# The back of a unit in another order: both turned halves copied ahead of the Silu pair, the centred product in one stage, squares summed by ScalarE

## The reference

```python
x = x + conv_ref(_ln_c(x), ...)        # the mixer, a Mamba block
t = t + ffn_ref(_ln_t(t), ...)         # mixture of 8 experts, top 1, with capacity 640

# conv_ref
x_norm = layer_norm(x_flat, ln_g, ln_b)
y = mamba_block(x_norm, ...)           # in_proj, conv of 4 taps, silu, delta = softplus(...), selective scan
                                       # with 16 states for each of 128 channels, times silu(z), out_proj
y = layer_norm(y + skip_scale * x_norm, ln_g, ln_b)
y = y @ proj_w.T + proj_b

# ffn_ref
logits = x @ gate_w + gate_b
probs = softmax(logits); idx = argmax(probs)
pos = running count of tokens of the same expert - 1;  kept = pos < C
y = expert MLP of the kept tokens, times prb
```

## Time and profile before

| | |
|---|---|
| median of 3 runs | 411.19 us (409.86 to 411.86) |
| the profiled execution | 404.2 us, of which 402.4 us are its span |
| granted clock of PE, mean | 0.866 of full speed |
| pass 1 (scans from 95.54 us) | rests on 100 to 172 us |
| pass 2 | some 172 to 237 us |
| pass 3 | 237.25 to 288.42 us |
| the last unit's scans | 289.6 to 311.4 us |

### The profile page before, as it was taken

The page is one execution under the profiler, slowest core; times in us unless marked ns, Lnnn a source line. Parts: engine busy times, 40 slices in busy tenths (PEclk is TensorE's granted clock), DMA queues, the critical chain, the costliest instruction groups (busy, mean ns, idle before and its releaser), DMA issues. The chain is left out here.

```text
span 402.4 us, 4213 instructions
## 1 busy us (share of the span) xinstructions
PE 314.5 (78%) x1257; PEld 187.1 (47%) x1257; DVE 316.0 (79%) x355; ACT 225.2 (56%) x398; POOL 269.3 (67%) x196
## 2 busy tenths in 40 slices
PE   8832988647988799898888959877678759999930
PEld 3311433113634355473434426544366536989920
DVE  4799998999997968999797899999997223565650
ACT  4456688718676944857885846455533226464410
POOL 3436847988564797688659768966588500777771
PEclk9975799998899955969996896999999559999975
DMA  5186999989987866588975638999801063000000
GB/s 105 29 290 242 266 294 402 374 201 377 368 261 285 241 197 252 195 247 280 329 241 187 222 135 281 284 329 340 156 21 31 15 189 81 9 16 17 21 11 0
DMA packets 43985, 78.67 MB, mean 195 GB/s; under 512 B 16051, under 2 KB 26094, under 8 KB 43963
## 3 DMA queue, kind: packets, MB, share of 16 engines
q1 hardware_dynamic: 41066, 73.88, 57.4%
q0 software_dynamic: 2896, 4.53, 4.0%
HBM read 72.30 MB, written 7.54 MB: 198 GB/s over the span
## 5 line engine op out<-in xcount | busy, mean ns | idle before, releaser
L481 POOL TENSOR_TENSOR prod<-h,csb 128x1024 f32<-128x1024 f32 (+1 forms) x64 | 142.0, 2221 | 55.5 <-DVE h L1217 33.4
L1217 DVE TENSOR_TENSOR_SCAN h<-dA,Bp 128x1024 f32<-128x1024 f32 (+1 forms) x64 | 137.7, 2151 | 4.8 <-ACT hl L661 1.4
L910 PE MATMUL Yp<-prod,ident 128*128 128x512 f32 (+1 forms) x256 | 128.3, 633 | 16.1 <-POOL prod L481 16.0
L647 ACT ACTIVATE dA<-delta,aneg 128x1024 f32<-128x1024 f32 (+1 forms) x64 | 69.0, 1090 | 29.8 <-DVE h L1217 25.5
L910 PEld LDWEIGHTS Yp<-prod,ident 128*128 128x128 f32 x256 | 50.0, 209 | 73.9 <-issue 46.5
L1187 DVE TENSOR_TENSOR Bp<-Cp,bsb 128x1024 f32<-128x1024 f32 (+1 forms) x64 | 74.6, 1166 | 3.5 <-DMA bsb<-bc_rows 1.4
L562 POOL DMA_INDIRECT out_dram<-dA,csb x30 | 30.7, 1023 | 28.1 <-DVE dA L1404 20.8
L520 POOL DMA_INDIRECT slots<-rows_,slot x30 | 30.1, 1005 | 7.2 <-issue 4.5
L1390 DVE TENSOR_TENSOR dA<-Bp,b2s 128x320 f32<-128x320 f32 x8 | 3.9, 491 | 26.2 <-PE Bp L1081 26.2
L1071 PE MATMUL Cp<-prod,w1s 128*128 128x384 f32 (+1 forms) x64 | 21.5, 459 | 0.0
L1081 PEld LDWEIGHTS Bp<-w2s,prod 128*128 128x128 f32 x160 | 19.0, 192 | 1.4 <-ACT prod L814 1.0
(11 more groups left out here) (276 smaller groups left out, 552.1 us busy)
## 6 DMA issues: line engine op xcount, KB each, us to landing
bsb<-bc_rows SPq DMA_DIRECT2D x48, 512.0 KB, 5.6
csb<-bc_rows SPq DMA_DIRECT2D x48, 512.0 KB, 5.8
bsb<-bc_rows SPq DMA_DIRECT2D x16, 384.0 KB, 4.7
csb<-bc_rows SPq DMA_DIRECT2D x16, 384.0 KB, 5.7
slots<-fill POOLq DMA_DIRECT2D x1, 2600.0 KB, 21.8
csb<-slots SPq DMA_DIRECT2D x6, 325.0 KB, 5.4
bcs<-bc_rows SPq DMA_DIRECT2D x2, 512.0 KB, 12.3
xs_in<-in_x_dram SPq DMA_DIRECT2D x1, 768.0 KB, 5.5
```

The costliest lines, as they stand in the source:

```text
L481: po.tensor_tensor(prod[:, k % 4, c], h[:, k % 3, c], csb[:, k % CSLOTS, c], ALU.mult).then_inc(s_pP, 1)
L647: ac.activation(dA[:, k % 3, c], at(delta, UNITS[v][0])[:, c], ACT.Exp, scale=aneg[:, n:n + 1]).then_inc(s_dA, 1)
L910: ins = te_.matmul(Yp[:, c], idn, prod[:, k % 4, c], start=False, stop=(n == 15), skip_group_check=True)
L1217: ve.tensor_tensor_scan(h[:, k % 3, c], dA[:, k % 3, c], Bp[:, c], 0.0, ALU.mult, ALU.add).then_inc(s_scan, 1)
```

## The change

For the units 0, 1 and 2 (`v < CARRY`) the helper `parts` puts both halves into one stage. ACT copies both halves of the first transposes in stage 5, ahead of the Silu pair; on PE the transposes of the second half and `add_state(v, 4)` come ahead of the first matmul of B and C in stage 5. The second copy of the second transposes (L690) moves ahead of `front`'s work of stage 9 on ACT. The centred product of all 8 tiles is made in stage 10 in one bank (`products_bank`), and its squares and copies follow in ACT's stage 10. The logits of these units go to `M1` (`logits`), and the wait for the raw gate's second copy moves from PE to DVE (L1250). In every unit ACT sums the squares itself: one activation with an accumulator output for each tile of 64 channels, in the place of one activation for 8 or 4 tiles and a reduce on DVE (L1231, L1245, both gone). The second inverse root moves from stage 13 to stage 12.

```diff
+        def products_bank(v, q, m):
+            if v < CARRY:
+                return M1[:, 4 * q * C:(4 * q + m) * C]
+            return turn_bank(v, q)[:, 0:m * C]
+        def parts(v, n, first):
+            if v < CARRY:
+                return (0, 1) if n == first else ()
+            return (n - first,) if n in (first, first + 1) and quad(v, n - first) else ()
+        def logits(v, nt):
+            return (M1 if v < CARRY else M0)[:, 0:nt * E]
...
@@ ScalarE, back @@
                 if n == 2:
                     act.wait_ge(b_op, v + 1)
-                    ac.activation(sq[:, 0:nt, :], tiles(mixer_bank(v)[:, 0:nt * C], C, nt), ACT.Square).then_inc(b_sq, 1)
+                    for t in range(nt):
+                        ins = ac.activation(sq[:, t, :], mixer_bank(v)[:, t * C:(t + 1) * C], ACT.Square, accum_out=bs[:, 0, t:t + 1])
+                    ins.then_inc(b_sq, 1)
...
-                if n in (5, 6) and quad(v, n - 5):
-                    q, w = n - 5, quad(v, n - 5) * P
+                for q in parts(v, n, 5):
+                    w = quad(v, q) * P
                     act.wait_ge(b_tr, quads(v) + q + 1)
...
-                if n in (10, 11) and quad(v, n - 10):
-                    q, m = n - 10, quad(v, n - 10)
-                    act.wait_ge(b_lg, quads(v) + q + 1)
-                    src = tiles(turn_bank(v, q)[:, 0:m * C], C, m)
-                    ac.activation(sq[:, 4 * q:4 * q + m, :], src, ACT.Square)
+                for q in parts(v, n, 10):
+                    m = quad(v, q)
+                    act.wait_ge(b_lg, quads(v + 1) if v < CARRY else quads(v) + q + 1)
+                    src = tiles(products_bank(v, q, m), C, m)
+                    for t in range(m):
+                        ac.activation(sq[:, 4 * q + t, :], src[:, t, :], ACT.Square, accum_out=bs[:, 10, 4 * q + t:4 * q + t + 1])
                     ac.activation(cg[:, 4 * q:4 * q + m, :], src, ACT.Copy).then_inc(b_cg, 1)
-                if n == 13:
-                    act.wait_ge(b_var3, v + 1)
+                if n == 12:
+                    act.wait_ge(b_cg, quads(v + 1))
                     inverse_root(10, nt).then_inc(b_rs3, 1)
...
@@ ScalarE, the loop over the stages @@
-                    if v and n < 8:
+                    if v and n != 8 and n < 10:
                         back(v - 1, n)
                     if v + 1 < B:
                         front(v + 1, n)
-                    if v and n >= 8:
+                    if v and (n == 8 or n >= 10):
                         back(v - 1, n)
...
@@ TensorE, the loop over the stages @@
                 for n in range(16):
+                    if n == 5:
+                        if v:
+                            back(v - 1, n)
+                        add_state(v, n - 1)
                     if v + 1 < B:
                         front(v + 1, n)
...
+                    if n == 5:
+                        continue
...
@@ VectorE, back @@
-                if n == 2:
-                    dve.wait_ge(b_sq, v + 1)
-                    ve.reduce_sum(bs[:, 0, 0:nt], sq[:, 0:nt, :], X).then_inc(b_var, 1)
...
-                if n == 12:
-                    dve.wait_ge(b_cg, quads(v + 1))
-                    ve.reduce_sum(bs[:, 10, 0:nt], sq[:, 0:nt, :], X).then_inc(b_var3, 1)
                 if n == 13:
                     link = Chain(dve, b_dve, v, 3)
                     dve.wait_ge(b_lgt, v + 1)
                     dve.wait_ge(b_rs3, v + 1)
+                    if v + 2 < B:
+                        dve.wait_ge(f_zr, 2 * (v + 2))
```

More of the change, by code:

```diff
@@ L230, in metaformer_layer @@
         s_mul, s_dA, s_scan, s_pP, s_sum, s_hl = map(sem, "s_mul s_dA s_scan s_pP s_sum s_hl".split())
-        (b_yg, b_op, b_sq, b_y2, b_var, b_rs, b_n2, b_tr, b_n2T, b_pr, b_t1, b_tr3, b_h3T, b_lg, b_cg, b_var3, b_rs3,
+        (b_yg, b_op, b_sq, b_y2, b_rs, b_n2, b_tr, b_n2T, b_pr, b_t1, b_tr3, b_h3T, b_lg, b_cg, b_rs3,
          b_lgt, b_h3, b_ld, b_ex, b_oh, b_base, b_acc, b_pos, b_prb, b_ids, b_idx, b_dve, b_dve2, b_dve3, b_res,
          b_sent) = map(sem, (
-             "b_yg b_op b_sq b_y2 b_var b_rs b_n2 b_tr b_n2T b_pr b_t1 b_tr3 b_h3T b_lg b_cg b_var3 b_rs3 "
+             "b_yg b_op b_sq b_y2 b_rs b_n2 b_tr b_n2T b_pr b_t1 b_tr3 b_h3T b_lg b_cg b_rs3 "
              "b_lgt b_h3 b_ld b_ex b_oh b_base b_acc b_pos b_prb b_ids b_idx b_dve b_dve2 b_dve3 b_res b_sent").split())
@@ L675, in back @@
                 if n == 3:
-                    act.wait_ge(b_var, v + 1)
+                    act.wait_ge(b_sq, v + 1)
                     inverse_root(0, nt).then_inc(b_rs, 1)
@@ L797, in _ @@
                 decay_last(n)
-            for n in (5, 6, 8, 9, 10, 11, 13, 14, 15):
+            for n in (5, 6, 8, 9, 10, 11, 12, 14, 15):
                 back(CARRY, n)
@@ L824, in dense_hidden @@
                               bias=b1c[:, j:j + 1]).then_inc(d_hid, 1)
-            for n in (2, 3, 5, 8, 10, 13, 14):
+            for n in (2, 3, 5, 8, 10, 12, 14):
                 back(LAST, n)
@@ L956, in back @@
                     ins.then_inc(b_tr3, 1)
-                if n in (10, 11) and quad(v, n - 10):
-                    q = n - 10
+                for q in parts(v, n, 10):
                     pe.wait_ge(b_h3T, quads(v + 1) if v < CARRY else quads(v) + q + 1)
-                    if q == 1 and v < CARRY:
-                        pe.wait_ge(b_cg, quads(v) + 1)
                     for t in range(quad(v, q)):
-                        ins = te_.matmul(turn_bank(v, q)[:, t * C:(t + 1) * C], bT[0:C, (4 * q + t) * P:(4 * q + t + 1) * P],
+                        ins = te_.matmul(products_bank(v, q, quad(v, q))[:, t * C:(t + 1) * C],
+                                         bT[0:C, (4 * q + t) * P:(4 * q + t + 1) * P],
                                          cen[:, :], start=True, stop=True)
@@ L966, in back @@
                 if n == 12:
-                    if v + 2 < B:
-                        pe.wait_ge(f_zr, 2 * (v + 2))
-                    if v == CARRY:
+                    if v <= CARRY:
                         pe.wait_ge(b_cg, quads(v + 1))
@@ L973, in back @@
                     for t in range(nt):
-                        ins = te_.matmul(M0[:, t * E:(t + 1) * E], bT[0:C, t * P:(t + 1) * P], ggw[:, :], start=True,
+                        ins = te_.matmul(logits(v, nt)[:, t * E:(t + 1) * E], bT[0:C, t * P:(t + 1) * P], ggw[:, :], start=True,
                                          stop=True)
@@ L1249, in back @@
                     dve.wait_ge(b_rs3, v + 1)
-                    link(ve.tensor_tensor(work(1, nt), work(0, nt), over(bs[:, 12, 0:nt], E), ALU.mult))
+                    if v + 2 < B:
+                        dve.wait_ge(f_zr, 2 * (v + 2))
+                    link(ve.tensor_tensor(work(1, nt), logits(v, nt).rearrange("p (t e) -> p t e", e=E),
+                                          over(bs[:, 12, 0:nt], E), ALU.mult))
                     link(ve.tensor_tensor(work(2, nt), work(1, nt), gb[:, :].unsqueeze(1).broadcast_to([P, nt, E]), ALU.add))
```

## The result

| | before | changed |
|---|---|---|
| median | 407.54 us (405.61 to 411.86, 14 runs) | 415.35 us (411.84 to 417.52, 14 runs) |
| ratio | 1 | 1.0176 [1.014, 1.0213] |
| profiled execution, span | 402.4 us | 414.5 us |
| mean granted clock of PE | 0.866 | 0.841 |

The change makes the kernel slower by 7.8 us. The forecast was +5.0 us on a median of 411.19; the 14 runs of the kernel before, three of which were the ones shown, have a median of 407.54.

The account below looks back on a forecast made before the run. No engine is full, so the order of waits bounds it, with PE's clock. Terms: +6.2 us by pass 2 (pass 1's +2 included), -1.2 in pass 3, so +5.0 on the 411.19 median: 416 us, range 405.5 to 421.

Parts of the forecast that it names:

- A: Stages 5 and 6: PE starves and its clock falls there; 416 us, between 413.5 and 422; chance 0.48.
- Some 7: DVE's wait at the residual, in us, if PE's clock falls; 4.6 if the clock holds.
- the residual is late by 1.6 + 1.7 + 1.0 = 4.3: Stages 5 to 8, us: first B and C copy late 1.6, slower projection 1.7, slower step-size matmul 1.0.
- the 6 us: Lateness of the step size's second half; half caught up, leaving the expert choice 3.7 late, some 2 reaching the next pass.
- Rival C: Stages 10 to 14: 2.19 us gap gone, PE stays at full speed if later idle is below some 2; 406 us; chance 0.24.
- The stall ahead of the gate's second half: PE idle for 4.9 us, waiting for ACT's first raw gate copy behind the squares; the clock taken to fall.
- the chosen 0.4: Price in us of one ACT square with accumulator, chosen between 0.15 and 0.6; eight take 3.2 us.
- If the squares cost under 0.2 us: ACT's squares: a sign that the prediction would be wrong; 0.4 us apiece was assumed.
- The cover of stage 2: 2.6 us more on ACT for squares, hidden by its 1.71 us wait for PE; uncovered, up to 2 us a pass.
- 3.7 late: Choice of the expert after stages 9 to 12: 160.6 against 156.9 us.
- The reduces: DVE's two removed reduces per unit: gain 1.2 us in pass 3, nothing in passes 1 and 2 or the last unit.
- PE's list: Stage 5: adding ahead of B and C gains PE nothing, as it was waiting for Silu then anyway.

Follow-up runs that it names:

- e1: Changed kernel with stage 5 as before on both ACT (second half copied behind the Silu pair) and PE (old list): ratio to the kernel before 0.9825.
- e2: Kernel before with only the stage 5 edit (both halves copied early, PE's new order): ratio to the kernel before 1.0265.
- e3: Changed kernel plus three useless matmuls of 512 columns on PE between the two halves of B and C: ratio to the kernel before 0.988.
- a2: Changed kernel, unedited, measured again on another chip: ratio to the kernel before 1.0155.
- e10: Changed kernel with the whole of stage 5 as before, repeated on another chip: ratio to the kernel before 0.9899, 402.64 us.
- e5: Changed kernel with stage 5 as before, and ACT's first raw gate copy moved ahead of the squares: ratio to the kernel before 0.9847.
- e6: Kernel before with only ACT's second copy of the second transposes moved ahead of front's stage 9 work: ratio 0.9837, from two executions.
- e4: Changed kernel with one activation for all squares, DVE's reduces and the second root in stage 13 as before: ratio to the kernel before 1.0205.
- e7: Changed kernel with stage 5 and the squares both as before: median 420.85 us beside 423.64 of the kernel before, or 0.993, no interval.
- e11: Changed kernel with ACT's second copy back in stage 6 and PE's new list kept, repeated on another chip: ratio 1.0045, 411.05 us.
- e8: Changed kernel with only ACT's second copy put back in stage 6, PE's new list kept: ratio to the kernel before 0.9995.
- e9: Changed kernel plus one useless matmul on PE between the two halves of B and C: ratio to the kernel before 1.0004, 1.011 by medians.

## Why the prediction was right in its case and too low in its sum

**The case was A, and its mechanism is shown.** Table load late (2.1 us by the working; 2.15 more between the first copied half's start and the load), two turned copies with an idle time of 1.56 us between them (1.5), then idle times of 1.38, 2.77 and 0.69 us on PE (1.4, 2.7, 0.7), the clock at one half in stages 6 to 8, the projection at 3.51 us (3.6) and the addition behind it at 3.73 (3.78). e1 and e2 put the loss in stage 5 from both sides; e3 shows that it is PE's clock that is paid for, not mainly ACT's lateness. The Trainium skill (TensorE: Matmul & The Clock Gate, What's actually happening) says that half speed is the default and activity releases it; e3, where added work raised the clock and made the kernel faster, agrees. That 415.35 lies so close to 416 is partly luck: the median it was put on was 3.65 us above that of the 14 runs, and the sum was 2.8 us too small.

**The residual's wait was under-sized.** "Some 7" measured 9.91 and 8.15 us. The term "the residual is late by 1.6 + 1.7 + 1.0 = 4.3" left out that the clock falls already within the second half of B and C: 2.08 us in place of 1.12, another 1.0. From the start of the first copied half to the end of the projection it took 12.11 us before (116.20 to 126.41 + 1.90) and takes 17.24 now (120.98 to 134.71 + 3.51): 5.1 us, where the working had 4.3. Pass 2's wait grew by 5.34 us, which is this. Pass 1's grew by 7.49, so that DVE came 2.4 us earlier against that copy, where the working had 0.6 for the reduce; in a2, the same kernel, the wait of pass 1 was 5.79.

**The step that failed is what the loss was set against.** The working had half of the 6 us "caught up because PE would otherwise be cold at 141 anyway", and nothing gained in stages 9 to 12. Undoing stage 5 alone shows the two terms apart: the rest of the change is worth a ratio of 0.9825 (e1) and 0.9899 (e10), that is 4 to 7 us to the better, and stage 5 costs 0.028 to 0.033 on top of it (1.0176 less 0.9899, 1.0155 less 0.9825): 11 to 14 us, where +5.0 was the sum of everything. The changed kernel and e1 never ran on one chip; a2 and e5, which did, are 0.031 apart. Both terms were too small by several us, and their errors partly cancelled, the cost being the one that was more off.

**Rival C's mechanism was there, too, and worked beside A's, though only in part as C had it.** Removing the idle time of 2.19 us made the second half of the centred product early in both passes, and e6 has that alone: 3.2 us by the passes of its profile, some 7 by its wide ratio. C gave 5 us for it, and that is the size. But C had it from a clock that stays at full speed through the stages 10 to 14 in place of 20.4 us at half. That was wrong on both sides. The 20.4 us stood in pass 1 only, pass 2 had 7; and in the changed kernel and in e1 PE's idle time ahead of the gate's second half is 3.27 and 3.28 us, above C's bound of 2, and the clock falls there, for 6 to 7 us in e1 and for 7 and 10 us in the two passes of the changed kernel. The gain comes all the same, because DVE's wait at the reduce (3.31 and 2.45 us) is gone and that at the choice is 0.54 and 0.51 us in e1. In treating A and C as alternatives the prediction missed that they lie in different stages and add up.

**The stall ahead of the gate's second half** was put at 4.9 us and is 3.27. The whole difference is the squares: just under 0.20 us apiece in place of the chosen 0.4, near the lower bound of 0.15. Eight of them are 1.6 us less, and 4.9 less 3.27 is 1.6. "If the squares cost under 0.2 us" was one of the prediction's own signs of being wrong, and it came in by a hair; what it was to decide, the gain in the stages 9 to 12, did turn out larger than the sum had it. The cover of stage 2 held: ACT still waits for PE in stage 4, 1.71 us at 118.82, just as before. The expert choice was expected "3.7 late"; its wait grew by 1.7 and 1.0 us, and pass 1 took 78.5 us in the profiled execution against 71.6 before.

**The reduces.** Forecast -1.2 us in pass 3: from the first scan of pass 3 to the first of the last unit it took 51.45 us before and 50.86 after, -0.6. That is no proof: without the reduces it also took 51.79 us in e1, 51.75 in e10 and 52.36 in e5, and with them 51.45 and 51.44 in e4 and e7. No gain from the reduces is shown.

**PE's list was priced at nothing** ("what PE gains by adding ahead of B and C is nothing") and was not weighed as a loss of its own. e11 against e10 is 0.0146, 6 us, for it (8.4 by the medians): with the addition moved out from between the two halves of B and C the idle time is 2.74 us in place of 1.09, without any help of the copy that ACT makes early. Of the 0.028 to 0.033 of stage 5 this is about half. The other half comes with ACT's copy, 0.011 to 0.018 by the changed kernel less e11 or e8 (1.0176 and 1.0155 against 1.0045 and 0.9995). The split can be taken in this order only: with PE's old list the second half's transposes stand behind the first matmul of B and C, which waits for Silu, so that ACT would wait for them ahead of Silu for ever, and no run can have ACT's copy alone. The copy makes everything 1.6 us later, and in the timelines there is a second idle time then, of 1.38 us, ahead of the first half of B and C, which e8 and e11 do not have. With it, and the 2.77 us behind it, (0.93 us in pass 1 of e2, 1.38 elsewhere) the clock was lost in both passes of all four profiles (the changed kernel, a2, e2, e4). That this idle time is what makes the difference is argued, not shown: the kernel before and e1 have it too, and e8 and e11 lost the clock without it in three passes of four.

**What stays open.** Why the clock fell behind 2.74 us of idle time in pass 1 of e11 and not in that of e8, with the same list. No length of idle time divides the passes in which it fell from the others: it also fell behind 1.09 us in pass 2 of e10, and in the kernel before it stood at half from about 171.7 us on, behind an idle time of 1.08 us that ended at 170.18:

```profile
171.70:178.50 6.80, 6.80 (x24) 0.50 0.77 236
```

What decides it, and how long half speed then lasts, the runs do not show. Why pass 2 waits longer at the residual than pass 1 in some executions of the same kernel (5.79 and 8.56 in a2, 9.91 and 8.15 here) wasn't tried either.

## What to carry to other kernels

A filler on PE between two dependent matmuls is not only throughput: in this kernel the additions that stood between the two halves of B and C kept the clock up in all passes looked at but one, and moving them out cost 6 to 8 us without a single instruction more. Before two matmuls are put side by side, look at what the second one waits for, and read the granted clock behind it. And where a change touches two places with an idle time each, price both and add them: the gain of one and the loss of the other are not rivals.

## What the runs showed of the hardware that was not expected

- An activation of 128x64 with an accumulator output shows as two instructions, of 0.20 and 0.19 us, which start 0.10 us apart; a tile costs 0.19 to 0.20 us of ACT's time in all. That is less than the scaled copy of one tile without a sum, 0.25 us.
- Three matmuls that compute nothing, six instructions and 2.74 us in each of two passes, brought the ratio to before from 1.0155 and 1.0176 to 0.988 (e3); one matmul, a pair of 1.02 us in the profile, brought it to 1.0004, or 1.011 by the medians (e9), and the clock was still lost behind the 1.91 us left idle.
- The same program kept the clock in one execution and lost it in another behind the same idle time of 2.74 us (e8, e11). Single executions of e8 lie between 402.54 and 412.03 us.
- How long half speed lasts differs within one kernel: before, 20.4 us in pass 1 with PE busy all the time, and 7 us at the same place in pass 2.
- Chips differ in a part of the kernel only: behind the first scan of the last unit it took 112.5 to 113.2 us on some and 125.0 to 131.1 on others, while the first scan of pass 1 came at 95.5 to 99.5 us on all.
